# Chunk 0's weight sums moved behind those of chunk 5 on GpSimd, their split moved two quads later

## What is computed

```
# layer 0
scale = cond @ norm_w.T + 1.0
h = x * (scale[:, None, :] * rsqrt(mean(x * x) + EPS))
u = h @ up_w.T                       # 512 -> 2 x 2048
val, gate = split(u, 2)
h = val * gelu(gate)
y = act_quant(h) @ weight_quant(down_w).T
x = y + x
# layer 1
Wd_b = Wd + ((h_lang @ Wdd.T + bdd) * 0.1).reshape(B, BN, D)
Wu_b = Wu + ((h_lang @ Wdu.T + bdu) * 0.1).reshape(B, D, BN)
x = x + relu(x @ Wd_b.T + bd) @ Wu_b.T + bu
```

## Time and profile before

| | us |
|---|---|
| median of 3 runs | 851.05 |
| lowest, highest | 850.76, 851.84 |
| profiled execution, its own time | 852.22 |
| span of the profiled execution | 850.3 |

### The profile page before, as it was taken

The page is one execution under the profiler, slowest core; times in us unless marked ns, Lnnn a source line. Parts: engine busy times, 40 slices in busy tenths (PEclk is TensorE's granted clock), DMA queues, the critical chain, the costliest instruction groups (busy, mean ns, idle before and its releaser), DMA issues.

```text
span 850.3 us, 11822 instructions
## 1 busy us (share of the span) xinstructions
PE 837.2 (98%) x3990; PEld 369.2 (43%) x3990; DVE 607.5 (71%) x913; ACT 389.0 (46%) x632; POOL 77.1 (9%) x79
## 2 busy tenths in 40 slices
PE   6999999999999999999999999999999999999998
PEld 5334444444434444444344444444444444444443
DVE  5997787989877865558776556668985664445986
ACT  5678887766454532227445542126433332224000
POOL 0463332302000000001000000000200000000100
PEclk9999999999999999999999999999999999999999
DMA  9879988666899853377898854436247444432232
GB/s 346 326 255 344 337 288 296 233 218 222 308 347 369 301 180 106 114 243 275 297 323 311 286 200 133 158 106 201 89 129 226 137 160 139 141 112 81 99 124 74
DMA packets 64426, 183.49 MB, mean 216 GB/s; under 512 B 7024, under 2 KB 8304, under 8 KB 64368
## 3 DMA queue, kind: packets, MB, share of 16 engines
q1 hardware_dynamic: 64080, 182.48, 61.7%
q10 hardware_dynamic: 288, 0.26, 0.1%
HBM read 152.31 MB, written 29.36 MB: 214 GB/s over the span
## 4 chain that ended last, share of the span: by engine, by line
PE 92%; DVE 1%; ACT 0%; issue 0%; DVEq 0%; ACTq 0%
PE aux_ps L1167 10%; PE b_ps L1074 9%; PE b_ps L1078 9%; PE b_ps L1076 9%; PE a_ps L1074 6%; PE a_ps L1078 6%; PE a_ps L1076 6%; PE aux_ps L1119 6%; PE aux_ps L1218 3%; PE aux_ps L1209 3%; PE c_ps L1078 3%; PE c_ps L1074 3%; PE c_ps L1076 3%; PE e_ps L1074 3%; PE e_ps L1078 3%; PE e_ps L1076 3%
## 5 line engine op out<-in xcount | busy, mean ns | idle before, releaser
L1567 DVE SCALAR_TENSOR_TENSOR h_ring<-v_sb,unscale,gelu 128x512 f32<-128x512 f32 x63 | 50.4, 800 | 101.0 <-ACT gelu L876 52.6
L852 ACT ACTIVATE b_ps<-a_ps 128x512 f32<-128x512 f32 x63 | 36.7, 582 | 141.9 <-PE a_ps L1078 141.9
L1074 PE MATMUL b_ps<-t_mov,u_l 128*128 128x512 f16 x252 | 95.5, 379 | 0.8 <-DVE c_ps L1528 0.8
L1078 PE MATMUL b_ps<-t_mov,u_l 128*128 128x512 f16 x252 | 95.5, 379 | 0.0
L1076 PE MATMUL b_ps<-t_mov,u_l 128*128 128x512 f16 x252 | 95.5, 379 | 0.0
L1591 DVE TENSOR_TENSOR hmax<-gelu,hmax 128x512 f32<-128x512 f32 x120 | 82.5, 688 | 7.4 <-ACT gelu L882 2.2
L1167 PE MATMUL aux_ps<-h_ring,wq 128*128 128x512 f16 x384 | 84.8, 379 | 0.0
L751 POOL PARTITION_ALL_REDUCE yscale<-hmax x8 | 17.9, 2267 | 601.9 <-DVE hmax L1591 601.2
L886 ACT ACTIVATE gelu<-h_ring 128x512 f32<-128x512 f32 x64 | 40.3, 630 | 56.6 <-DVE h_ring L1567 56.6
L882 ACT ACTIVATE gelu<-h_ring 128x512 f32<-128x512 f32 x64 | 40.3, 629 | 51.5 <-DVE h_ring L1577 51.3
L1577 DVE SCALAR_TENSOR_TENSOR h_ring<-b_ps,unscale,gelu 128x512 f32<-128x512 f32 x64 | 47.9, 749 | 18.9 <-PE b_ps L1078 18.6
(11 more groups left out here) (220 smaller groups left out, 1627.9 us busy)
## 6 DMA issues: line engine op xcount, KB each, us to landing
w_ring<-in_Wdu SPq DMA_DIRECT2D x64, 512.0 KB, 6.1
w_ring<-in_Wdd SPq DMA_DIRECT2D x56, 512.0 KB, 7.0
u_l<-ul_dram SPq DMA_DIRECT2D x48, 512.0 KB, 4.6
u_e<-ue_dram SPq DMA_DIRECT2D x48, 384.0 KB, 3.1
h_ring<-in_up_w SPq DMA_DIRECT2D x16, 512.0 KB, 6.3
x_sb<-in_x SPq DMA_DIRECT2D x8, 1024.0 KB, 8.0
res<-in_down_w SPq DMA_DIRECT2D x16, 512.0 KB, 7.2
ul_dram<-u_l SPq DMA_DIRECT2D x15, 512.0 KB, 5.4
```

Source lines behind the costliest of these rows:

```text
L1074: pe.matmul(ps[:, :], weight(n, p, 0, k), hi, start=fresh and k == 0, stop=False, skip_group_check=True)
L1078: mm = pe.matmul(ps[:, :], weight(n, p, 1, k), hi, start=False, stop=k == 1, skip_group_check=True)
L1567: dve.scalar_tensor_tensor(out=h_slot(n)[:, TB:TS], in0=val[:, :], scalar=unscale[:, s // 2, j:j + 1], in1=gelu2[:, :], op0=ALU.mult, op1= ...
```

## The change

GpSimd's order of chunks becomes 1, 2, 3, 4, 5, 0, 6, ... (was 1, 2, 3, 0, 4, 5, 6, ...). Chunk 0's sums wait for nothing but their raw chunk. Chunk 6 puts its sums in slot 8 of `h_ring` instead of 19, and so waits for the eighth low part of the moving operand (`s_tlo`, which frees the slot) instead of for `sums_low`; that wait passes to chunk 8, the next in slot 19. The split of chunk 0's sums, on ACT and on DVE, goes from the end of quad 3 to the end of quad 5, and `put_sums` from j = 4 to j = 6 on SP. Nothing is added or removed, and TensorE's queue is the same.

```diff
-SUM_ORDER = (1, 2, 3, 0) + tuple(range(4, NP))
+SUM_ORDER = (1, 2, 3, 4, 5, 0) + tuple(range(6, NP))
...
-            total = yscale[:, :] if j % 2 else h_ring[:, {2: 12, 4: 15}.get(j, SUM_SLOT), :]
+            total = yscale[:, :] if j % 2 else h_ring[:, {2: 12, 4: 15, 6: 8}.get(j, SUM_SLOT), :]
...
-                    if j == 4:
+                    if j == 6:
                         put_sums()
...
-                elif j == 0:
-
-                    pool.wait_ge(s_seed_c, 1)
                 elif j >= 3:
                     if j == 6:
+
+                        pool.wait_ge(s_tlo, 8)
+                    elif j == 8:
                         pool.wait_ge(s_sums_lo, 2)
                     pool.wait_ge(s_ulo, part_count(j - 2, 3))
...
-                if n == 3:
+                if n == 5:
                     sums_high(0)
                     sums_high(1)
...
-                if n == 3:
+                if n == 5:
                     sums_low(0)
                     sums_low(1)
```

## The result

| | before | changed |
|---|---|---|
| median us (21 runs each) | 851.82 | 853.40 |
| lowest to highest | 850.41 to 852.87 | 852.33 to 854.59 |
| ratio, 95% interval | | 1.0017 (1.0012 to 1.0023) |
| span of the profiled execution | 850.3 | 850.9 |

852.0 against a median of 851.05 had been forecast, that is +0.93.

What follows compares the result with a forecast made beforehand. TensorE, busy 98% of the span, was taken to bound the kernel. Terms -0.92 (quad 2) and +1.85 (quad 6) sum to +0.93 us, giving 852.0 us against the median of 851.05; range 850.1 to 853.4.

Steps and rivals of the forecast that it cites:

- the likeliest case: Whole kernel: the terms sum to +0.93 us, 852.0 us, counted as "same"; chance 0.62, own range 851.3 to 852.5.
- rival 3: After quad 6's stall TensorE runs for a while at half pace: 1.4 us more, 853.4 us, slower; chance 0.07.
- a new wait in quads 3 to 5: Sign in the new profile that would show the prediction wrong: a TensorE wait turning up there; no size given.
- Quad 2, -0.92: Product 7: with POOL idle beside DVE, `seed_c(2)` ends earlier and the whole 0.92 us stall goes.
- the transfers as cause: Quad 2: alternative that DMA transfers, not POOL, slow DVE; the stall would then stay, a gain of 0.
- Quads 3 and 4, 0: Chunk 0's sums slow three DVE instructions by 1.4 us, covered by 1.87 us of idle time and departed split: 0.
- Quad 6, product 6, +1.16: ACT's split directly ahead of `seed_b(6)`, with 0.06 us slack, makes product 6 start 1.16 us later.
- Quad 6, product 7, +0.69 more: DVE's low parts of chunk 6 come 2.82 us late, so product 7 loses 1.85 us in all, including 1.16.
- my upper end: Quad 6, product 7: loss of 2.4 us if late sums slow two more instructions by 0.3 each.
- Afterwards, and SP: 0: After quad 6 both engines recover; on SP `put_sums` falls where the queue had nothing to issue: 0.
- The granted clock: Argument against the half pace: ahead of quad 2's 0.92 us stop, which did not bring it, the clock was 1.00.
- Rivals 1 and 2: First: quad 6 hides the split, 850.1, chance 0.13. Second: quad 2 keeps its stall, +1.85 alone, 852.9, chance 0.12.

Runs made afterwards that it cites:

- experiments 1: Changed kernel with GpSimd's order as before, only the split and `put_sums` in their new places; ratio 1.0031, +2.6 us against the kernel before.
- experiment 4: Changed kernel with chunk 4's sums held back until the eighth low part of the moving operand; ratio 1.0024, +2.0 us against the kernel before.
- experiment 5: Changed kernel with VectorE's half of the split moved behind quad 6's running maxima; ratio 1.0005, +0.4 us against the kernel before.
- experiment 3: Kernel before with chunk 0's sums behind chunk 4's and held until `seed_c(2)`; ratio 0.9990, -0.85 us against the kernel before.
- experiment 6: Changed kernel with both halves of the split later in quad 6; ratio 0.9994, -0.5 us against the kernel before.

## Why the prediction came out as it did

The direction and the two large mechanisms were right: GpSimd's sums made the stop of quad 2, and the moved split made both stops of quad 6. One term was put at nothing for a wrong reason, one was too small, and both errors point the same way. +0.93 was forecast and +1.45 measured, on the upper end of the likeliest case's own range (851.3 to 852.5, or +0.25 to +1.45). The absolute time fits less well: 853.40 stands on the upper end of the whole range (853.4), which was drawn for rival 3, the half pace, and that did not come. 0.77 of the distance is the kernel before itself, whose median was 851.05 in three runs and 851.82 in 21. That the absolute number is within the range is therefore in part luck. And by its own list the prediction was wrong in one place: it named a new wait in quads 3 to 5 as a sign, and one of 0.30 us turned up in quad 4.

- **Quad 2, -0.92**: right as priced; the stop went away whole, and by GpSimd, as experiments 1 and 4 show by the pair's 2.35 us. By the Trainium skill (SBUF — State Buffer, section SBUF: two separate sides) GpSimd and VectorE hold one port pair in turn. The trace agrees in which instructions are slowed (1.21 against 0.75 us with both tensors in SBUF, no change with one in PSUM); the holding itself no run shows. The choice against the transfers as cause was the right one. But the reason was told too narrowly: I made chunk 4's sums, as neighbours of the last instructions, the cause. Experiment 4 put them back there without a stop. In the places tried, the count of GpSimd's instructions beside an unbroken stretch of VectorE is what matters.
- **Quads 3 and 4, 0**: wrong, 0.30. I had priced the slowing nearly right (1.4 us for three instructions; 2.11 + 1.21 against 1.48 + 0.75 is 1.1), but covered it with the idle time and the old split, which stand *behind* these three instructions, on the way to the low parts 2 and 3 of chunk 4 (`u_l`). The low part 1 of chunk 4 is one of the three itself, and product 5 reads it first. The step that failed is "so the low parts of chunk 4 start no later": true of parts 2 and 3, not of part 1, whose reader I did not look up.
- **Quad 6, product 6, +1.16**: measured 1.17, in experiment 5 alone 1.18.
- **Quad 6, product 7, +0.69 more**: measured 1.01. DVE's delay up to the low parts was right (its wait for ScalarE is 1.41 us, the low parts start 2.07 behind ScalarE's start). Mis-sized was what follows: I took over the durations of before (0.60 and 1.10), while the sums of chunk 8, released by the late low parts, covered both instructions (0.95 and 1.21), 0.46 us more. This stood in my upper end (2.4 in all; 2.18 came). The sum itself was also rounded up on the way: 96.27 + 2.82 - 0.37 + 0.69 + 0.15 - 97.75 is 1.81, not 1.85.
- **Afterwards, and SP: 0**: right. No stop follows until product 5 of quad 10, which had one before (0.32 in both).
- **Rival 3, the half pace**: did not come; behind a stop of 1.17 us the next matmul follows at 0.21 us (93.77 to 93.98). The granted clock that I had set against it decides nothing: it reads 1.00 over 18 to 21 us as well, where the matmuls stood 0.42 us apart. The distance between starts decides. Rivals 1 and 2 fell as well: the split found no slack, and the stop of quad 2 did not stay.

## What to carry to other kernels

When every engine feeds one that never rests, price a moved step at the first instruction behind it that the full engine reads, in each queue by itself, and give slack only to what stands between the two: idle time that lies behind that instruction covers nothing. Work that is off the critical path may still be best where it was: the same split cost nothing ahead of `seed_b(4)`, 2.2 us ahead of `seed_b(6)`, and about 0.1 a few instructions later. And an idle-looking helper engine that slows its neighbour belongs into stretches in which the neighbour waits anyway; here a wait that holds GpSimd *back* made the kernel faster.

## What the runs showed of the hardware

- GpSimd's sums slow only some of VectorE's instructions. The multiplication with both tensors in SBUF (L1567) took between 0.74 and 1.30 us in the first step, that with one tensor in PSUM (L1577) never more than 0.75; in experiment 3 it took 0.74 at 55.76, with chunk 0's sums running beside it from 55.60. The lines of one instruction each (least/median/greatest ns) in the kernel before, 40 to 170 us:

```profile
L1567 DVE SCALAR_TENSOR_TENSOR h_ring<-v_sb,unscale,gelu x11: 737/1101/1302, 55.1 to 158.9; 128x512 f32<-128x512 f32 x11
...
L1577 DVE SCALAR_TENSOR_TENSOR h_ring<-b_ps,unscale,gelu x12: 735/742/753, 39.9 to 160.1; 128x512 f32<-128x512 f32 x12
```

- I had not expected the slowing of an instruction with a single tensor input: the first running maximum (L1588, one SBUF input and a constant) took 0.41 us with GpSimd idle (experiment 4, at 48.94) and 0.95 beside it (changed kernel, at 48.77). It is not slowed each time: in the kernel before it took 0.41 at 52.54, while GpSimd's sums followed one another.
- The slowing can repeat to a hundredth of a us (the pair and the multiplication took 2.35 and 1.21 us in the kernel before and in experiments 1 and 4), but it hangs on how the instructions meet: the same pair took 1.88 us in experiment 6, with one of chunk 4's sums beside it, and L1508 took 1.22 to 1.77 us beside chunk 3's sums. A price per instruction (0.47 us here) is good for a sum over several, to some tenths.
